# Gated cross-attention and a mixture of experts on one core: first masks in six pieces, a later query transposition, eleven early tiles from twelve batches

## The reference, cut to what matters

```python
def _L0_xattn_ref(input, memory, mask, w_input, dot_scale):
    input_dot = jnp.einsum('bqd,od->bqo', input, w_input)
    cross_dot = jnp.einsum('bqd,bkd->bqk', input * dot_scale, memory)
    att = input_dot + cross_dot - 1e+30 * mask[:, None, :]
    return jnp.einsum('bqk,bkd->bqd', jax.nn.softmax(att, axis=-1), memory)

def _moe_forward(x, W_router, W_gate, W_up, W_down):
    probs = jax.nn.softmax(jnp.einsum('bsd,ed->bse', x, W_router), axis=-1)
    gates, indices = jax.lax.top_k(probs, 2)
    gates = gates / jnp.sum(gates, axis=-1, keepdims=True)
    # per expert: silu(x @ wg) * (x @ wu), then @ wd, weighted by its gate and summed

x = x + jnp.tanh(g_xattn[0]) * _L0_xattn_ref(_layernorm(x), ctx_1024, mask, w_input, dot_scale)
x = x + jnp.tanh(g_ffn[0]) * _L0_ffn_ref(_layernorm(x), w_router, w_gate, w_up, w_down)
```

## Time and profile before

| | |
|---|---|
| Time, three runs | 278.66, 282.87 and 322.13 us, median 282.87 |
| Profiled execution | 280.85 us, its span 278.8 us |
| PE busy | 242.4 us of the span (87%) |
| DVE, ACT, POOL busy | 144.4, 137.0, 112.2 us |
| DMA | 36.49 MB, 131 GB/s over the span |
| Granted TensorE clock, mean | 0.946 |

### The profile page before, as it was taken

How to read it: one execution, slowest core, us unless ns; L and a number is a source line. 1 busy time by engine, 2 the same in 40 slices (tenths; PEclk the granted TensorE clock), 3 DMA queues, 4 the chain that set the end, 5 groups by cost and what they waited for, 6 DMA issues and landing times.

```text
span 278.8 us, 5798 instructions
## 1 busy us (share of the span) xinstructions
PE 242.4 (87%) x1614; PEld 198.3 (71%) x1615; DVE 144.4 (52%) x467; ACT 137.0 (49%) x302; POOL 112.2 (40%) x197
## 2 busy tenths in 40 slices
PE   6799999999999999999978599699999999998100
PEld 6557777788777788777778387588888888887100
DVE  3434666767777767787746338223433343432024
ACT  3445455676555686655545234345545555545000
POOL 3250432157644476636374535433424223233200
PEclk9989999999999999999979979989999999999855
DMA  5875787778787888888632003221211111000164
GB/s 134 223 199 149 186 218 195 187 210 228 200 244 210 214 191 207 206 218 225 246 76 49 15 2 91 63 70 58 58 39 45 54 38 38 28 19 31 34 218 119
DMA packets 17645, 36.49 MB, mean 131 GB/s; under 512 B 3692, under 2 KB 9460, under 8 KB 17620
## 3 DMA queue, kind: packets, MB, share of 16 engines
q1 hardware_dynamic: 13580, 31.36, 43.4%
q0 software_dynamic: 2560, 3.77, 4.5%
q10 hardware_dynamic: 1480, 1.05, 1.2%
HBM read 30.89 MB, written 5.27 MB: 130 GB/s over the span
## 4 chain that ended last, share of the span: by engine, by line
PE 70%; DMA 8%; issue 6%; DVE 5%; ACT 4%; POOL 4%; SPq 0%; POOLq 0%; DVEq 0%; ACTq 0%
PE psum L1067 14%; PE psum L1046 13%; PE psum L1170 9%; PE psum L1022 7%; PE psum L1148 6%; PE psum L1150 5%; PE psum L1149 5%; PE psum L1159 4%; DMA ctx_sb<-results 3%; PE psum L1057 2%; DMA slots<-pair_rows,slot_i 2%; ACT probsT L616 2%; POOL slots L527 2%; DMA results<-y_sb,dest 2%; ACT qT L611 1%
## 5 line engine op out<-in xcount | busy, mean ns | idle before, releaser
L583 POOL DMA_INDIRECT results<-y_sb,dest x32 | 30.7, 959 | 57.1 <-DVE dest L948 25.6
L1067 PE MATMUL psum<-ctx_sb,probsT 120*100 120x128 f32 (+1 forms) x384 | 49.2, 280 | 0.0
L959 DVE SCALAR_TENSOR_TENSOR scores<-probs,row_in,psum 128x512 f32<-128x512 f32 x32 | 23.9, 747 | 42.6 <-ACT probs L691 41.3
L1067 PEld LDWEIGHTS psum<-ctx_sb,probsT 120*100 120x100 f32 (+1 forms) x384 | 44.9, 172 | 0.3 <-issue 0.2
L1046 PE MATMUL psum<-ctxT,qT 128*100 128x512 f32 (+1 forms) x96 | 43.2, 587 | 0.0
L527 POOL DMA_INDIRECT slots<-pair_rows,slot_i x32 | 33.5, 1046 | 22.6 <-DVE slot_i L846 8.4
L691 ACT ACTIVATE probs<-psum 128x512 f32<-128x512 f32 x32 | 19.1, 598 | 39.0 <-PE psum L1150 39.0
L1170 PE MATMUL psum<-w_down,hidT 128*128 x256 | 34.3, 277 | 0.8 <-ACT y_sb L706 0.6
L782 DVE CUSTOM_DVE_ANT_0 scores<-psum,maskb 100x1444 f32<-100x1444 f32 x16 | 26.6, 1660 | 13.3 <-PE psum L1046 13.3
L1170 PEld LDWEIGHTS psum<-w_down,hidT 128*128 128x128 f32 x256 | 31.5, 194 | 1.2 <-issue 1.2
L1148 PE MATMUL psum<-w_hi,rowT_hi 128*128 x64 | 29.1, 454 | 2.4 <-issue 1.0
(11 more groups left out here) (138 smaller groups left out, 372.2 us busy)
## 6 DMA issues: line engine op xcount, KB each, us to landing
ctx_sb<-in_ctx SPq DMA_DIRECT2D x16, 720.0 KB
maskb<-mask_scaled SPq DMA_DIRECT2D x14, 564.1 KB
w_raw<-in_w_experts SPq DMA_DIRECT2D x16, 256.0 KB, 6.0
row_in<-slots SPq DMA_DIRECT2D x32, 65.0 KB, 1.9
w_down<-in_w_experts SPq DMA_DIRECT2D x4, 512.0 KB, 9.2
ctx_sb<-results SPq DMA_DIRECT2D x4, 200.0 KB
ctx_sb<-results ACTq DMA_DIRECT2D x4, 200.0 KB
out<-x_all SPq DMA_DIRECT2D x4, 200.0 KB
```

The lines of the kernel that those rows point to most:

```text
L583: nc.gpsimd.indirect_dma_start(results, bass.IndirectOffsetOnAxis(ap=dest[:, s:s + 1], axis=0), y_sb[:, s, :], None).then_inc(y_stored[s], 16)
L1067: last = nc.tensor.matmul(attn_ps[0:Q, 0:D], probsT[0:rows[c], c, :], ctx_sb[0:rows[c], b % RING, c, :], start=(c == 0), stop=(c == CHUNKS ...
```

## The change

- **First masks.** The masks of batches 0 and 1 come in pieces of 512 keys, six pieces as six rows, loaded twice (32 rows and again 6), so that one row group holds the rounded and one the remaining part; one matmul per piece adds both, three a batch for six. The full mask is loaded, scaled and stored after that, behind the first evictions, and the fourth context load goes behind the first spread mask. Five of the keep-warm products at the start go, and `tanh` moves behind the first exponential.
- **Query.** `transpose_q(b + 1)` moves from ahead of the transposed probabilities to behind the first attention group, and its copy on ACT from ahead of the copies of the probabilities to just ahead of the exponential. It now waits for the eviction of the context whose PSUM bank it shares.
- **Between the stages.** `step(15)` on PE no longer holds tokens and router product of batch 13; the whole last attention product stands ahead of the first expert tile. POOL scatters batch 10 ahead of the last normalisations and changes the order of the others.
- **Early tiles.** Twelve batches (`EARLY_PART` 5) give `EARLY` 11 tiles. The early tables are made in steps 14 and 15 of DVE, and the late tables in four parts behind tiles 4 to 7.
- **Tails.** `tail_row` is taken from the part before the last, so a cleared region has 328 rows, 82 partitions with 4 rows each, and is stored ahead of the scatters of batches 14 and 15, for which POOL waits. All eight clears are issued on SP, two each behind the row loads of tiles 3 to 6.
- **Result scatters** of the last four tiles no longer wait for the one before.

The core of the diff:

```diff
-EARLY_PART = 4
-EARLY = 8
+EARLY_PART = 5
+EARLY = 11
...
-SP_TAILS = 6
+TAIL_ROWS = 328
+TAIL_PART = 82
...
-        empty = sb("empty", [P, ROW])
+        empty = sb("empty", [P, SPREAD, ROW])
...
-        select = sb("select", [B, MASKED, Q], F32R)
-        mask_hi = w_hi[0:B, 0:K]
-        mask_lo = w_lo[0:B, 0:K]
+        first_rows = LOW + MASKED * PIECES
+        select = sb("select", [first_rows, MASKED * PIECES, Q], F32R)
+        first_raw = w_lo[0:first_rows, 0:PIECE].bitcast(F32)
+        first_split = w_hi[0:first_rows, 0:PIECE]
...
+            pieces = mask.rearrange("b (t n) -> (b t) n", n=PIECE)
             load_x(0)
-            sp.dma_start(mask_rows, mask).then_inc(mask_raw, 16)
+            sp.dma_start(first_raw[0:LOW, :], pieces[0:LOW, :]).then_inc(first_loaded_mask, 16)
+            sp.dma_start(first_raw[LOW:first_rows, :], pieces[0:MASKED * PIECES, :]).then_inc(first_loaded_mask, 16)
             load_ctx(0)
             load_x(1)
+            sp.dma_start(mask_rows, mask[:, 0:K]).then_inc(mask_raw, 16)
             load_ctx(1)
             load_x(2)
             load_ctx(2)
-            load_ctx(RING - 1)
             sp.wait_ge(mask_stored, 16)
             load_mask(MASKED)
+            load_ctx(RING - 1)
...
-                    sp.wait_ge(tails_stored, 16 * E)
...
-                at = sp.value_load(tail_row[0:1, e:e + 1], min_val=0, max_val=DUMMY)
-                sp.dma_start(slots[bass.ds(at, P), :], empty[:, :]).then_inc(tails_stored, 16)
+                at = sp.value_load(tail_row[0:1, e:e + 1], min_val=0, max_val=DUMMY - TAIL_ROWS)
+                sp.dma_start(slots[bass.ds(at, TAIL_ROWS), :].rearrange("(p r) d -> p r d", r=SPREAD),
+                             empty[0:TAIL_PART, :, :]).then_inc(tails_stored, 16)
 
             sp.wait_ge(early_ready, 1)
             sp.wait_ge(scattered[0], 16 * 2 * PARTS[EARLY_PART][1])
             for n in range(LOOP):
                 load_rows(0, n)
-                if n == EARLY - 1:
+                if n == 3:
                     sp.wait_ge(tails_ready, 1)
-                    for e in range(SP_TAILS):
-                        clear_tail(e)
+                if 3 <= n < 3 + E // 2:
+                    clear_tail(2 * (n - 3))
+                    clear_tail(2 * (n - 3) + 1)
...
+                if b == B - 1:
+                    scatter(b - 5)
...
-                if b == B - 2:
-                    pair_landed(0)
-                if B - 2 <= b:
-                    scatter(b - 4)
...
-            pair_landed(1)
-            scatter(12)
+            scatter(11)
             root2(B - 2)
             normalise2(B - 2)
+            pair_landed(0)
+            scatter(12)
+            root2(B - 1)
+            normalise2(B - 1)
             pair_landed(1)
             scatter(13)
-            root2(B - 1)
-            normalise2(B - 1)
             last_gates()
+            pool.wait_ge(tails_stored, 16 * E)
...
-                if k % 2 == 0:
+                if k % 2 == 0 and k < LOOP_END:
...
-                if 0 <= b - 1 < B:
-                    if b + 1 < B:
-
-                        act.wait_ge(probsT_raw, (b - 1) * GROUPS + 1)
-                        copy_qT(b + 1)
+                if b >= 1:
                     for g in range(GROUPS):
                         copy_probsT(b - 1, g)
-                elif b == 0:
-                    copy_qT(1)
                 if b + 1 < B:
                     evict_ctxT(b + 1, 0)
                     evict_ctxT(b + 1, 1)
-                if 0 <= b - 2 < B - 2:
+                if 0 <= b - 2 < B - 3:
                     copy_xn2T(b - 2)
+                if b + 1 < B:
+                    copy_qT(b + 1)
                 if b < B:
                     act.wait_ge(negmax_done, b + 1)
                     nc.scalar.activation(probs[0:Q, :], scores[0:Q, :], ACT.Exp, bias=negmax[:, b % 2:b % 2 + 1],
                                          accum_out=rowsum[:, b % RING:b % RING + 1]).then_inc(probs_done, 1)
+                    if b == 0:
+                        act.wait_ge(small_loaded, 48)
+                        nc.scalar.activation(tanh_g[:, :], gates_in[:, :], ACT.Tanh).then_inc(tanh_done, 1)
...
+            act.wait_ge(first_loaded_mask, 32)
+            nc.scalar.activation(first_split, first_raw, ACT.Copy, scale=NEG).then_inc(mask_hi_done, 1)
+            copy_qT(0)
+            evict_ctxT(0, 0)
+            evict_ctxT(0, 1)
             act.wait_ge(mask_raw, 16)
             nc.scalar.activation(mask_rows, mask_rows, ACT.Copy, scale=NEG).then_inc(mask_scaled_done, 1)
             act.wait_ge(mask_scaled_done, 1)
             act.dma_start(mask_scaled, mask_rows).then_inc(mask_stored, 16)
-            copy_qT(0)
-            nc.scalar.activation(mask_hi, mask_rows, ACT.Copy).then_inc(mask_hi_done, 1)
-            evict_ctxT(0, 0)
-            evict_ctxT(0, 1)
-            act.wait_ge(small_loaded, 48)
-            nc.scalar.activation(tanh_g[:, :], gates_in[:, :], ACT.Tanh).then_inc(tanh_done, 1)
...
+                if k == EARLY - 1:
+                    rowT_high(i, k + 1)
...
-            exp_gap(LAST - 1)
-            rowT_high(0, 0, first_rowT_ps)
-            nc.scalar.activation(warm[:, :], wi_col[:, :], ACT.Silu)
+            copy_xn2T(B - 3)
             for g in range(GROUPS):
                 copy_probsT(B - 1, g)
-            over_tiles(act, tile_step, between)
+            exp_gap(LAST - 1)
+            nc.scalar.activation(warm[:, :], wi_col[:, :], ACT.Silu)
+            rowT_high(0, 0, first_rowT_ps)
+            rowT_high(0, 1)
+            over_tiles(act, tile_step)
...
+                if p == LAST - 1:
+                    nc.vector.tensor_copy(tail_row[:, :], at[:, N, :]).then_inc(tails_ready, 1)
                 if p == LAST:
-                    nc.vector.tensor_copy(tail_row[:, :], at[:, N, :]).then_inc(tails_ready, 1)
...
-                if b >= 2:
+                if 2 <= b < B - 1:
                     top_two(b - 2)
-                if 3 <= b and b % 2 == 1:
+                if 3 <= b < B - 1 and b % 2 == 1:
                     choose((b - 3) // 2)
-                if b == 12:
+                if b == 14:
+                    tile_counts(False)
                     tile_runs(False)
-                if b == 14:
-                    tile_tables(False)
+                if b == B - 1:
+                    tile_experts(False)
+                    tile_rows(False)
...
-            nc.vector.tensor_tensor(mask_lo, mask_rows, mask_hi.bitcast(F32), ALU.subtract).then_inc(mask_lo_done, 1)
+            nc.vector.scalar_tensor_tensor(out=first_split[LOW:first_rows, :], in0=first_raw[LOW:first_rows, :], scalar=NEG,
+                                           in1=first_split[LOW:first_rows, :].bitcast(F32), op0=ALU.mult,
+                                           op1=ALU.subtract).then_inc(mask_lo_done, 1)
...
-                if k == 0:
-                    rowT_low(i, 1)
-                    residual(B - 1)
-                    statistics2(B - 1)
...
-                if n == 3:
+                if n == 4:
+                    tile_counts(True)
+                if n == 5:
                     tile_runs(True)
-                if n == 4:
-                    tile_tables(True)
+                if n == 6:
+                    tile_experts(True)
+                if n == 7:
+                    tile_rows(True)
...
             residual(B - 2)
+            statistics2(B - 2)
+            attention_gain(B - 1)
+            top_two(B - 3)
+            choose(LAST - 1)
+            place(LAST - 1)
+            gate_pair(LAST - 1)
+            residual(B - 1)
             rowT_low(0, 0, first_rowT_ps)
-            statistics2(B - 2)
-            gate_pair(LAST - 1)
-            place(LAST - 1)
-            attention_gain(B - 1)
+            statistics2(B - 1)
+            rowT_low(0, 1)
...
                 pe.wait_ge(xn_done, b + 1)
+                wait(pe, ctxT_act, 2 * b + 1 if b else 0)
...
-                for n in range(0, K, 512):
-                    m = min(512, K - n)
-                    nc.tensor.matmul(scores_ps[0:Q, n:n + m], select[:, b, :], mask_hi[:, n:n + m], start=True, stop=False)
-                    nc.tensor.matmul(scores_ps[0:Q, n:n + m], select[:, b, :], mask_lo[:, n:n + m], start=False, stop=False)
+                for t, n in enumerate(range(0, K, PIECE)):
+                    m = min(PIECE, K - n)
+                    nc.tensor.matmul(scores_ps[0:Q, n:n + m], select[:, b * PIECES + t, :], first_split[:, 0:m], start=True, stop=False)
...
-                    transpose_probs(b - 1, b + 1 < B)
-                else:
-                    pe.wait_ge(ctxT_act, 1)
-                    transpose_q(1)
+                    transpose_probs(b - 1)
                 if b + 1 < B:
                     transpose_ctx(b + 1)
-                if b == 0:
-                    keep_warm(4)
                 if 4 <= b and b % 2 == 0:
                     ranks((b - 4) // 2)
```

(62 more changed lines are left out.)

63 lines of the change are left out of this document (33 added, 30 removed).

## The result

The changed kernel takes **292.31 us** (median of 4 runs, 290.47 to 296.75) against 281.19 for the kernel before (4 runs). The ratio of the times is 1.04, with a 95% interval of 1.034 to 1.046: slower, and outside the range of the prediction. The profiled execution took 293.99 us around a span of 292.0.

A forecast was written before the change was run, and what follows sets the result against it. PE was taken as the bound, with 70% of the chain. From 280.85 us, start -5.2, attention steps -1.8, transition +8.8 and end -1.1 gave 281.5 us; range 275 to 291, the forecast's own part 277 to 285.

The forecast's parts named there:

- the transition: Stretch from the last scores to tile 8, 136.40 to 184.54 us before: tile 8 forecast 8.8 us later.
- The head: Start up to the third scores: masks ready earlier, first scores about 10.4 us instead of 12.36; gain 5.2 us.
- The clock rival: First scores: PE idles about 1 us ahead, the clock falls, costing 1.7 us (283.2); some 40% within the forecast's range.
- The clears: Between the stages: each 82-partition clear lies on two DMA engines, 3.9 us each, 31.2 for eight, delaying row loads.
- The steady step: Attention steps: context transposes start earlier with the query copy behind; net 0.14 us a step, 1.8 us over 13.
- The end: Result scatters of the last tiles: without the wait for the one before, a gain of 1.1 us.
- Wide clears: Rival: a clear goes over ten or more engines, all eight take under 7 us and are hidden; 264.2 us, 13%.
- The row loads don't queue behind the clears: Rival: clears still on two engines, but tiles 4 to 10 run freely and row 11 is late; 278.6 us, 10%.
- Small pieces: Rival: each engine writes 520 bytes at a time, 5.05 us a clear, 40.4 in all; 290.7 us, 13%.

## Why the prediction was wrong

**The step that failed** is the sentence of the transition that reads "Results pile up on POOL until 195, but it clears two per 4.4 us and PE makes two per 5.9, so it has caught up by tile 24". The date was right (the first result was scattered at 194.54), the conclusion wasn't. I had asked whether POOL would be late at the end, and not who waits for a result to have landed before that. DVE does: the destinations of tile 8 go into the place that the scatter of result 0 reads. Everything that DVE does for later tiles stands behind that wait. So the tiles behind tile 8, which the forecast left at 67.5 us, cost **7.8 us** more in the trace, and a ring of 16 takes 8.4 us out of them. Even as a sum it was wrong: with some seven results waiting at 195 (my estimate), POOL at two in 4.4 us and PE at two in 5.9, POOL gains one in 8.7 us and needs until tile 29. The ring of eight and DVE's wait are in the code of before; there result 0 was scattered at 175.8, ahead of tile 8 at 184.5, so the wait never showed.

**The head was mis-sized**: -5.2 forecast, +0.7 measured. The steps behind the context's arrival were right: with late small loads and the context at 8.77 instead of 10.10, scores 1, 2 and 3 started at 11.25, 16.85 and 24.55, all some 1 us behind my 10.4, 15.9 and 23.5. What failed is the premise "the context evictions set the start of the scores", which took the context's landing from the trace of before. I moved the mask pieces and knew of the small loads on ACT, but didn't ask which load now sits in the slow stretch of the DMA engines; that it exists was to be seen at 6 to 8 us in before, behind the first context. The clock rival (+1.7) is part of this: 13.81 to 21.80 between the first two scores in the changed kernel, 11.25 to 16.85 with full clock. And most of the 5.2 us wasn't to be had in these runs: 3.9 and 4.8 us at the head were worth 1.1 and 1.6 us in the time, within what the runs vary, since the attention stage meets its second limit.

**The clears were right**, in mechanism and in size, and this was no luck: two engines, forecast from the counts of packets for 100 and 128 rows, 3.8 us a clear (3.9 forecast), three waits of PE for rows 5 to 7, and tile 8 55.3 us behind the last scores (56.9 forecast). The Trainium skill's rule (DMA: Bandwidth & Descriptors, "Why a DMA increments its semaphore by 16 and not by 1"), the largest divisor up to 16, agrees with all four shapes here: 1, 2, 4 and 14 engines for 83, 82, 92 and 84 partitions.

**The steady step** gained 0.20 us, not 0.14: 13 steps in 105.1 us. **The end**: the wait was worth 0.5 us at the last scatter and not 1.1, as ACT's copies of results (POOL waits 0.75 us for the last one) pace it as soon as the old wait doesn't; I had counted the whole of one wait, without what comes next. The changed kernel has these 0.5 us too (its last scatter is 7.9 us behind the start of tile 31, 8.4 before), but from there to the end it took 18.9 us against 18.4, so the row of the table shows 0.0. That last part varies from 18.0 to 19.5 us between the runs, for a reason that none of them shows.

**The rivals.** "Wide clears" stood at 264.2; the profiled execution with 84 partitions took 275.9 us. By the cuts of the table, my sum against that run: third scores 23.5 against 28.3, 13 steps 105.9 against 107.6 (with waits for contexts), the stage to tile 8 39.6 against 42.0, tiles 8 to 31 67.5 against 69.9 (the destination ring again), the end 25.7 against 26.1. Narrow against wide clears, rings of eight, is thus 13.3 us up to tile 8 and 5.4 behind it, where I had 17.3 and nothing. "The row loads don't queue behind the clears" falls: the waits for rows 5, 6 and 7 follow the clears 7.4 and 14.8 us apart. "Small pieces" falls too: 2080 bytes a packet; that 290.7 comes close to the result is an accident.

## What to carry to other kernels

For every transfer that is moved or made late, list who waits for the reuse of its buffer, not only who reads what it brings; a ring's wait that never showed in a trace had slack, and the change may use it up. Give a DMA a partition count with a large divisor up to 16: 84 instead of 82 partitions was worth 5% here. And before a stage is started sooner, look at the second resource that fills it: here, at a DMA share of 0.85 beside a full PE, a gain at the head of the stage was mostly returned in it.
